# Graph kernel: the edge attributes' maximum is taken beside the input normalisation, and the attribute products run one chunk behind the duplicate search

## The reference

```
h = (feat - mean) * rsqrt(var + eps) * gamma + beta      # layer 0: input normalisation
a_in  = segment_sum((h @ W_in  + b_in )[src] * iw, dst)   # weighted adjacency
a_out = segment_sum((h @ W_out + b_out)[dst] * ow, src)   # its transpose, other weights
...                                                       # gates, residual, layernorm
# layer 1, three times:
msg = x[src] + edge_attr @ We.T + be
agg = segment_sum(msg, dst) / max(deg, 1)                 # needs sum of edge_attr by dst
x   = relu(agg @ Wl.T + bl + x @ Wr.T)
# layers 2 and 3: graph convolutions with the degree, then batch norm
```

## Time and profile before

| | us |
|---|---|
| median of three runs | 3275.62 |
| the profiled execution | 3277.98 |
| its span, first to last instruction | 3276.2 |
| granted TensorE clock, mean over the span | 0.936 |

### The profile page before, as it was taken

How to read it: one execution, slowest core, us unless ns; L and a number is a source line. 1 busy time by engine, 2 the same in 40 slices (tenths; PEclk the granted TensorE clock), 3 DMA queues, 4 the chain that set the end, 5 groups by cost and what they waited for, 6 DMA issues and landing times.

```text
span 3276.2 us, 37001 instructions
## 1 busy us (share of the span) xinstructions
PE 2563.7 (78%) x14593; PEld 1400.9 (43%) x14593; DVE 1677.4 (51%) x1848; ACT 1262.3 (39%) x2535; POOL 801.4 (24%) x611
## 2 busy tenths in 40 slices
PE   0551057777777777888888889998999999999896
PEld 0320023333333333444444434555565664555543
DVE  3441679999999995554555545112012324132313
ACT  0137057777777504666666523101001111121203
POOL 3000467777777731222222200000000000000000
PEclk9885579999999999999999999999999999999897
DMA  9999843333333317889888652644434326454362
GB/s 373 404 387 409 255 92 58 58 58 58 58 57 54 33 13 187 214 212 228 216 215 215 168 131 47 135 92 90 99 81 101 83 71 128 103 122 100 79 145 66
DMA packets 326008, 466.24 MB, mean 142 GB/s; under 512 B 106089, under 2 KB 261992, under 8 KB 325604
## 3 DMA queue, kind: packets, MB, share of 16 engines
q1 hardware_dynamic: 246445, 420.30, 47.5%
q0 software_dynamic: 57360, 0.92, 4.8%
q10 hardware_dynamic: 22023, 42.59, 4.0%
HBM read 313.97 MB, written 149.75 MB: 142 GB/s over the span
## 4 chain that ended last, share of the span: by engine, by line
PE 42%; DMA 19%; POOL 11%; SPq 11%; DVE 8%; issue 6%; ACT 3%; DVEq 0%; ACTq 0%; POOLq 0%
PE psum L1046 24%; POOL cell_mat L511 11%; PE psum L994 11%; DMA cell_mat<-ROW 10%; SPq L344 10%; DMA Q<-cell_mat 8%; PE psum L926 3%; DVE AR L1330 3%; DVE Q L1395 2%; ACT Q L660 2%; PE psum L1063 1%; DMA cell_mat<-SA 1%; PE psum L1073 1%; DVE ROW L1389 1%; ACT Q L651 1%
## 5 line engine op out<-in xcount | busy, mean ns | idle before, releaser
L1046 PE MATMUL psum<-FR 125*128 125x500 f16 (+1 forms) x4200 | 823.2, 355 | 20.8 <-DVE FR L1449 20.8
L511 POOL DMA_INDIRECT cell_mat<-ROW x391 | 618.8, 1582 | 538.4 <-DMA cell_mat<-SA 324.0
L896 PE MATMUL psum<-AR,Q 128*128 128x500 f16 (+1 forms) x2737 | 593.3, 356 | 183.8 <-DVE AR L1330 180.0
L1330 DVE TENSOR_SCALAR AR<-Q,ROW 128x3125 f16<-128x3125 f16 x391 | 721.4, 1901 | 7.5 <-PE psum L896 0.9
L1046 PEld LDWEIGHTS psum<-FR 125*128 125x128 f16 x4200 | 387.6, 98 | 429.9 <-issue 45.3
L896 PEld LDWEIGHTS psum<-AR,Q 128*128 128x128 f16 x2737 | 237.3, 98 | 455.8 <-DVE AR L1330 182.4
L1476 DVE SCALAR_TENSOR_TENSOR Q<-psum,small,ROW 128x1000 f32<-128x1000 f32 (+1 forms) x42 | 48.2, 1147 | 713.4 <-PE psum L1046 713.4
L1395 DVE SCALAR_TENSOR_TENSOR Q<-Q,small 125x1000 f16<-125x1000 f32 (+1 forms) x175 | 248.9, 1426 | 267.4 <-ACT Q L660 267.2
L660 ACT ACTIVATE Q<-Q,small 125x1000 f16<-125x1000 f32 (+1 forms) x175 | 262.3, 1499 | 121.5 <-DMA Q<-cell_mat 121.0
L940 PE MATMUL psum<-Q,FR 125*128 125x500 f16 (+1 forms) x1050 | 240.8, 368 | 73.1 <-DVE Q L1395 71.2
L994 PE MATMUL psum<-wl,Q 128*125 128x256 f32 (+1 forms) x1100 | 286.8, 401 | 5.7 <-ACT Q L717 3.0
(11 more groups left out here) (271 smaller groups left out, 2331.6 us busy)
## 6 DMA issues: line engine op xcount, KB each, us to landing
cell_mat<-SA SPq DMA_DIRECT2D x39, 3000.0 KB, 31.6
Q<-cell_mat SPq DMA_DIRECT2D x150, 703.1 KB
FR<-count_mat SPq DMA_DIRECT2D x180, 585.9 KB
AR<-cell_rows ACTq DMA_DIRECT2D x47, 640.0 KB, 4.1
count_mat<-Q SPq DMA_DIRECT2D x150, 117.2 KB
AR<-in_edge_attr SPq DMA_DIRECT2D x13, 960.0 KB, 4.8
Q<-in_edge_attr SPq DMA_DIRECT2D x48, 256.0 KB, 4.2
cell_mat<-ROW POOLq DMA_INDIRECT x391, 3.1
```

What stands on the lines that cost most here:

```text
L511: pool.indirect_dma_start(out=cell_mat, out_offset=bass.IndirectOffsetOnAxis(ap=at[c % VALS][:, k:k + 1], axis=0), in_=vals[c % VALS][:, k ...
L896: last = pe.matmul(a, own_attr, onehot[t % 3][:, t0:t0 + nt], start=t == 0, stop=t == ET - 1, skip_group_check=True)
L1046: last = pe.matmul(a[:, hh, 0:w], parts[:, c, t, f], slot(m, j)[:, i_, :], start=t == 0 and c == 0, stop=t == NT - 1 and c == 1, skip_grou ...
L1330: dve.tensor_scalar(onehot[t % 3], iota16, dst_c[:, t:t + 1], None, ALU.is_equal).then_inc(S["onehot_ready"], 1)
```

## The change

The attribute maximum moves to the front of the program: POOL, not SP, issues its 13 loads, into another pair of buffers, and DVE reduces them right after the normalisation. The scale is computed there too. POOL also takes over the store of `Xn` to `h_d` and the attribute loads of the first seven chunks (`EARLY`), all ahead of the scatter in its program. `LAG_C` goes from 6 to 1, so the products run 8 slots behind the search instead of 48; the ring of values grows from 6 to 14 chunks. The row loads of a chunk are cut into five DMAs of two rows, issued at five different tiles, and SP's attribute loads are cut in two, the second with a wait of its own.

```diff
-    LAG_C = 6
+    LAG_C = 1
-    VALS = 6
+    VALS = 14
-    PEAK_SLOT, SCALE_SLOT = 37, 38
+    EARLY = 7
+    ROW_PARTS = ((0, 2), (2, 4), (4, 6), (6, 8), (8, 10))
+    ROW_AT = {0: 0, 1: 1, 3: 2, 4: 3, 5: 4}
...
-        peak_buf = [AR[:, s * PEAK_TILES * EA:(s + 1) * PEAK_TILES * EA] for s in range(2)]
+        peak_buf = [FR[:, 6600 + s * PEAK_TILES * EA:6600 + (s + 1) * PEAK_TILES * EA] for s in range(2)]
...
 # SP, after the zeroing (the maximum's loads and h_d are gone from here)
-            sp.wait_ge(S["feat_split"], 2 * PIECES)
...
-            for c in range(CH):
-                if c >= 2:
-                    sp.wait_ge(S["attr_lo"], c - 1)
-                else:
-                    sp.wait_ge(S["scale_a_ready"], 1)
+            for c in range(EARLY, CH):
+                sp.wait_ge(S["attr_lo"], c - 1)
                 n = min(EC, EM - EC * c)
-                sp.dma_start(attr32[c % 2][:, 0:n], attr_main[:, EC * c:EC * c + n, :]).then_inc(attr_in[c % 2], 16)
+                sp.dma_start(attr32[c % 2][:, 0:4], attr_main[:, EC * c:EC * c + 4, :]).then_inc(attr_in[c % 2], 16)
+                sp.wait_ge(S["onehot_ready"], EC * (c - 3) + 9)
+                sp.dma_start(attr32[c % 2][:, 4:n], attr_main[:, EC * c + 4:EC * c + n, :]).then_inc(attr_in[c % 2], 16)
...
 # POOL, ahead of its wait for "zeroed"
+            for i in range(PEAK_LOADS):
+                if i >= 2:
+                    pool.wait_ge(S["peak_read"], i - 1)
+                pool.dma_start(peak_buf[i % 2]..., attr_main[:, i * PEAK_TILES:(i + 1) * PEAK_TILES, :]).then_inc(peak_in[i % 2], 16)
...
+            pool.wait_ge(S["feat_split"], 2 * PIECES)
+            for lo, hi in ((0, K0), (K0, P)):
+                pool.dma_start(by_node(h_d)[lo:hi], Xn[lo:hi]).then_inc(S["h_kept"], 16)
+            pool.wait_ge(S["h_kept"], 32)
+            for c in range(EARLY):
+                if c >= 2:
+                    pool.wait_ge(S["attr_lo"], c - 1)
+                pool.dma_start(attr32[c % 2], attr_main[:, EC * c:EC * c + EC, :]).then_inc(early_in[c % 2], 16)
...
 # ACT
+                if n == PIECES:
+                    act.wait_ge(S["peak_read"], PEAK_LOADS + 1)
...
-                if k == 1 and 0 <= c + 1 < CH and c:
-                    load_rows(c + 1)
+                if k in ROW_AT and c and c + 1 < CH:
+                    load_rows(c + 1, ROW_AT[k])
...
 # DVE: the blocks of slots 37 and 38 move ahead of the features' maximum and of their split
-                if t == PEAK_SLOT:
...
-                if t == SCALE_SLOT:
...
```

More of the change, by code:

```diff
@@ L278, in build_gnn @@
         attr_in = [sem(f"attr_in{s}") for s in range(2)]
+        early_in = [sem(f"early_in{s}") for s in range(2)]
         landed = [sem(f"landed{s}") for s in range(2)]
@@ L574, in _, with load_rows @@
                 now = slice(g * ROWS, (g + 1) * ROWS)
+                if n == PIECES:
+                    act.wait_ge(S["peak_read"], PEAK_LOADS + 1)
                 act.activation(feat[b][:, now, 0], Bn[b][:, now], ACT.Copy, scale=scale0[0:P, 0:1]).then_inc(S["feat_hi"], 1)
             act.wait_ge(S["feat_split"], 2 * PIECES)
-            def load_rows(c):
+            def load_rows(c, part):
                 if c >= 2:
                     act.wait_ge(S["abs_done"], EC * (c - 1))
-                a, b = max(EC * c - 1, 0), min(EC * c + EC + 1, ET)
-                i_ = a - (EC * c - 1)
-                act.dma_start(rows[c % 2][:, i_:i_ + b - a], cell_rows[a:b, :].unsqueeze(0).to_broadcast([128, b - a, 128])).then_inc(rows_in[c % 2], 16)
+                first = EC * c - 1
+                a, b = max(first + ROW_PARTS[part][0], 0), min(first + ROW_PARTS[part][1], ET)
+                if a < b:
+                    act.dma_start(rows[c % 2][:, a - first:b - first], cell_rows[a:b, :].unsqueeze(0).to_broadcast([128, b - a, 128])).then_inc(rows_in[c % 2], 16)
             for c in range(2):
-                load_rows(c)
+                for part in range(len(ROW_PARTS)):
+                    load_rows(c, part)
             def distance(t):
@@ L589, in distance @@
                 if k == 0:
-                    act.wait_ge(rows_in[c % 2], 16 * (c // 2 + 1))
+                    act.wait_ge(rows_in[c % 2], 16 * sum(EC * q - 1 + lo < ET for q in range(c % 2, c + 1, 2) for lo, _ in ROW_PARTS))
                 if t >= 2:
@@ L609, in attr_hi @@
             def attr_hi(c):
-                act.wait_ge(attr_in[c % 2], 16 * (c // 2 + 1) + (16 if c == CH - 1 else 0))
+                if c < EARLY:
+                    act.wait_ge(early_in[c % 2], 16 * (c // 2 + 1))
+                else:
+                    act.wait_ge(attr_in[c % 2], 32 * len(range(EARLY + (c - EARLY) % 2, c + 1, 2)) + (16 if c == CH - 1 else 0))
                 if c >= 2:
@@ L862, in _ @@
             pe.matmul(trp[:, 0, 0:2], ident[0:1, 0:1].to_broadcast([1, 128]), power2[0:1, :], start=True, stop=True).then_inc(S["tr_done"], 1)
+            pe.wait_ge(S["tr_read"], TR_AT["peak2"])
+            pe.wait_ge(S["peak_a_ready"], 1)
+            pe.transpose(trp[0:1, 0, 0:128], peak_a, ident[:, :]).then_inc(S["tr_done"], 1)
+            pe.wait_ge(S["tr_read"], TR_AT["peak_a"])
+            pe.matmul(trp[:, 1, 0:1], ident[0:1, 0:1].to_broadcast([1, 128]), power_a[0:1, :], start=True, stop=True).then_inc(S["tr_done"], 1)
             def claim(t):
@@ L1266, in _ @@
             dve.wait_ge(S["stat"], 3)
+            for i in range(PEAK_LOADS + 1):
+                dve.wait_ge(peak_in[i % 2], 16 * (i // 2 + 1))
+                n, v = (128, peak_buf[i % 2]) if i < PEAK_LOADS else (TAIL, peak_buf[i % 2][0:TAIL, 0:EA])
+                dve.tensor_reduce(peaks_a[0:n, 0, i:i + 1], v, AX.X, ALU.max)
+                last = dve.tensor_reduce(peaks_a[0:n, 1, i:i + 1], v, AX.X, ALU.min)
+                last.then_inc(S["peak_read"], 1)
+            dve.wait_ge(S["peak_read"], PEAK_LOADS + 1)
+            link(dve.tensor_scalar(peaks_a[:, 1], peaks_a[:, 1], -1.0, None, ALU.mult))
+            dve.tensor_reduce(peak_a, peaks_a, AX.XY, ALU.max).then_inc(S["peak_a_ready"], 1)
             for g in range(PIECES):
```

47 lines of the change are left out of this document (13 added, 34 removed).

## The result

The changed kernel takes 3244.76 us (median of 4 runs, 3238.17 to 3249.63) against 3276.66 us before (4 runs, 3275.25 to 3277.95): ratio 0.9897, 95% interval 0.9885 to 0.991. It gains 32 us where the forecast was 69. "Scatter", "row load" and "part" are used as ahead of the prediction; a landing is the end of a DMA's writing, for which somebody waits. The profiled run is 3246.2 us with a span of 3244.4.

What follows compares the result with a forecast made beforehand. DVE's one-hots and, nearly as late, POOL's scatter bound the kernel; afterwards the scatter: start 407, 766 us of steps, landed by 1176 instead of 1245, 69 us less: 3209 profiled, 3207 us median, range 3178 to 3258.

Steps and rivals of the forecast that it cites:

- What would bound it: End of the stage: the scatter on POOL, landed by 1176 us, replaces DVE's one-hots; the cells' load starts 69 us earlier.
- The maximum: Front part, DVE's reductions: from 142.4 to 225 us, bounds 196 and 243; the split then ends at 273.
- First attributes: Behind POOL's store of `Xn` beside the zeroing: store landed by 311 us, first attribute load 318, one-hots from 328.
- The loop: DVE-bound as before at 16.62 us a chunk: 812 us, last one-hot at 1140.
- The scatter's start: POOL's first scatter, after the zeroing (406 us) and the seventh attribute load (403): taken as 407.
- The scatter's pace: POOL's steps beside the row loads: 1.96 us each, bounds 1.85 and 2.105; 391 steps take 766 us.
- sign of being wrong: In the profile after: mean scatter steps above 2.05 us, among other signs, would show the forecast wrong.
- The stalls stay: Rival, chance 0.12: scatter pace stays 2.105 since the same bytes pass; 12 us less, 3264.
- Each small load stalls a scatter: Rival, chance 0.08: every part holds up a scatter; pace 2.43 at half today's stall each, 115 us more, 3391.

Runs made afterwards that it cites:

- rows in one load: The changed kernel with one row load of ten rows per chunk instead of five of two rows: 3235.73 us (0.988).
- TensorE's rows: The changed kernel without row loads: TensorE transposes a spread column of cell numbers and ScalarE copies the row from PSUM: 3185.72 us (0.9729).
- read from 16 places: The changed kernel with the table of rows stored 16 times, each row part read from 16 places for eight partitions each: 3263.31 us (0.9969).
- with 2/7 of the bytes gone: The changed kernel without the attribute loads from the eighth chunk on, only the five row parts left beside the scatter: 3231.78 us (0.9882).
- spare loads: TensorE's rows, with the five row loads a chunk issued again in their old slots into columns nobody reads: 3273.07 us (1.0001).
- spare attributes: TensorE's rows plus, from the ninth chunk, five unread 128 KB attribute loads a chunk: from one place 3232.93 us, from 16 places 3184.37 us.
- the load on four engines: Row part in the changed kernel with four copies of the table of rows, one place read for 32 partitions: 3341.63 us (1.0208).
- the four copies: The changed kernel with four copies of the table of rows, the six extra stores behind the copies of the weights: 3341.63 us (1.0208).

## Why the prediction was right and wrong

- **What would bound it: right.** The scatter is the new end, DVE's one-hots are not, and the time saved in the stage (1244.8 - 1210.8 = 34) is, but for 2 us, the time saved in the whole (32): the rest of the span takes 2033.6 us where it took 2031.4.
- **The maximum: nearly right.** Its end was forecast at 225, measured 235. Of the 10 us, 5 are the normalisation, which ends at 147.1 instead of 142.4; the rest is a pair of loads at 13.8 us instead of 13.1. The split ends at 283 instead of 273, the same 10 us.
- **First attributes: right to 8 us, but in part by luck.** The store of `Xn` was issued at 283.3 and landed at 315.6, 32 us for a forecast 38. Its terms were not what the forecast took. It was counted as 3125 packets of 1 KB, as SyncE's store in the kernel before is in the trace; from GpSimd it goes as 785 packets of 4 KB, from 288.3 to 314.3. They came at 30 a us and not 90; one takes some 0.2 us where a packet of 1 KB in the earlier trace rows takes 0.05, and the row parts share the engines as a third queue. A quarter of the packets at a third of the rate, and 5 us from the issue to the first one, make nearly the same sum. The turns themselves were as the earlier trace rows showed, here with three queues (290 to 300 us: store, zeroing, row parts):

```profile
q0 software_dynamic: 393, 1.60, 47.5%
q1 hardware_dynamic: 423, 1.66, 44.3%
q10 hardware_dynamic: 425, 0.39, 11.1%
```

  The Trainium skill's rule (DMA: Bandwidth & Descriptors, Queues, rings and completion order), by which each DMA engine takes turns between its queues, agrees with that. Low attributes came at 330.5 (forecast 319), one-hots at 335.7 (328). A term was missing: the first row parts land up to 24 us after issue beside the zeroing, and ScalarE waited 37.1 us for them in all.
- **The loop: right.** 16.62 us a chunk, last one-hot at 1147 (forecast 1140, with the 7.7 us of the late start).
- **The scatter's start: 8 us early of its forecast.** 399.0 against 407; the maximum's loads cost 29 instead of 34.
- **The scatter's pace: wrong, the step that failed.** The mechanism was the forecast's own (landings held up by row loads), and only the size of this term was off: I took 1.96 "nearer to the pace without row loads, since a stall comes only where a landing is later than two steps of POOL". Over the whole scatter it was (1207.3 - 399.0) / 390 = 2.073. That is 390 x (2.073 - 1.964) = 43 us more, less the 8 of the earlier start: the 34 us by which the end is late. Splitting a row load makes more and shorter waits, 139 instead of 60, with no gain in the sum. The forecast's own sign of being wrong, steps above 2.05 us in the mean, is what came. What it missed is that a part is not a fifth of a load: a load of ten rows from one place is under way for 2.65 us (rows in one load, 500 to 900 us), a part of two rows for 1.72, so five parts are 8.6 us. The forecast's pace came only where the row loads were gone (TensorE's rows, 1.93 and 3186 us) or read from 16 places (1.960).
- **The rivals.** "The stalls stay" is what happened. Its 3264 was too high by 19: it kept 407 for the start (8 us) and 2.105 for all 391 steps, where the last 50 go at 1.85 since loads end with the search. "Each small load stalls a scatter" did not happen, since five parts cost no more than one load of ten. The 0.12 that "the stalls stay" had was too little, but its only argument, that the same bytes pass, was no better than mine: with 2/7 of the bytes gone the pace stayed. Neither named what the runs found, the single place that is read.

Shown is that the row loads slow the scatter (taken away: 1.93; put back as spare loads: 2.08) and that the single place is what counts in loads of 128 KB (spare attributes from one place 2.115, from 16 places 1.947). Argued, and not shown, is that the way goes through the time for which a load is under way. It fits the table, the load on four engines (1.99 us, pace 2.201), and the one of ten rows, which comes once a chunk with 2.65 us and costs about the same (2.097) as five of 1.72. No run varied that time alone, and why one place takes longer stays open.

## What to carry to other kernels

Splitting a transfer that disturbs another engine's DMAs moved the disturbance about here and did not remove it; ask how long its packets are under way and what kind of access it is, and whether an engine with time left can make the data (here 0.30 us of TensorE and 0.28 us of ScalarE a tile for some 50 us in all). A pace taken from a stretch without the disturbance is a bound and no forecast. And work moved beside a saturated queue was paid by that queue and by whoever waited for it: 2.2 us for each load of 960 KB.

## What was not expected of the hardware

- Loads that give all 128 partitions the same 1 KB take 55 to 62 ns a packet and slow an accumulating scatter from 1.93 to 2.08 to 2.12 us a step. The same loads from 128 or 16 places take 48 to 49 ns and leave it at 1.95. From one place a load is under way for 1.64 to 1.80 us, from 16 or 128 for 0.82 to 0.89.
- A load split over 4 or 16 places takes ScalarE 0.51 to 0.54 us to issue, where the plain one takes 0.33; beside the zeroing the first ten of the four copies took 61.6 us, ten plain ones 14.3.
- The same 3.2 MB store goes as 3125 packets of 1 KB from SyncE and as 785 of 4 KB from GpSimd.
- Even with no other load in the loop the scatter's pace is 1.918, not the 1.85 of the stretch behind it.
